# Moving the experts' input norm and slot filling into self-attention, turning the router product round, and spreading the last layer norms over the end

## The reference

```python
x = _layernorm(x + gated_linear_recurrence(x))      # Wi, Wf, Wg, scan, Wo
x = _layernorm(x + cross_attention(x, ctx))          # 32 heads, 1601 keys
x = _layernorm(x + ffn(x))
# ffn(x): causal self-attention, then experts
h = _rms(x, w_ln1); ...                              # 16 heads of 32, rotary
x = x + ctx @ wo
h = _rms(x, w_ln2)
probs = softmax(h @ w_router); top 2 of 8 experts
routed = sum of the two experts' silu(h Wg) * (h Wu) Wd, by their weight
sh = the same with a shared expert, times sigmoid(h @ w_sh_eg)
x = x + routed + sh
```

## Time and profile before

| | us |
|---|---|
| median of 2 runs (2838.88 to 2840.54) | 2839.71 |
| the profiled execution | 2848.1 |
| its span, first to last instruction | 2846.2 |
| PE busy | 2557.4 |
| DVE busy | 1292.0 |
| ACT busy | 1386.4 |

### The profile page before, as it was taken

The page is one execution under the profiler, slowest core; times in us unless marked ns, Lnnn a source line. Parts: engine busy times, 40 slices in busy tenths (PEclk is TensorE's granted clock), DMA queues, the critical chain, the costliest instruction groups (busy, mean ns, idle before and its releaser), DMA issues. The chain is left out here.

```text
span 2846.2 us, 39040 instructions
## 1 busy us (share of the span) xinstructions
PE 2557.4 (90%) x15648; PEld 1591.7 (56%) x15648; DVE 1292.0 (45%) x1943; ACT 1386.4 (49%) x1691; POOL 826.0 (29%) x489
## 2 busy tenths in 40 slices
PE   7996869999999999999968999985699988889996
PEld 5874624443444344432235556544577888888775
DVE  5666723333333333320035565542434566666574
ACT  3221046667666766689964334323312355545221
POOL 2225735441544154410014333311330011111130
PEclk9997979999999999999989999996699999999998
DMA  4002646554554545364421000005451265565330
GB/s 163 15 1 87 201 102 169 151 141 98 154 159 121 125 125 168 100 152 114 114 72 55 1 1 1 1 1 219 158 203 32 96 208 198 200 214 184 111 107 30
DMA packets 205683, 323.98 MB, mean 114 GB/s; under 512 B 68800, under 2 KB 122048, under 8 KB 203456
## 3 DMA queue, kind: packets, MB, share of 16 engines
q1 hardware_dynamic: 190448, 253.46, 30.8%
q0 software_dynamic: 15056, 68.03, 6.8%
HBM read 217.82 MB, written 103.61 MB: 113 GB/s over the span
## 5 line engine op out<-in xcount | busy, mean ns | idle before, releaser
L698 ACT ACTIVATE c_prob<-c_psum 128x1024 f32<-128x1024 f32 x832 | 815.1, 1036 | 292.6 <-PE c_psum L852 212.7
L676 POOL TENSOR_TENSOR c_rr<-c_ms,c_half 128x32 f32<-128x32 f32 x68 | 372.8, 5484 | 399.2 <-DVE c_ms L712 399.2
L869 PE MATMUL c_psum<-c_prob,c_vq 128*17 128x512 f32 x3328 | 439.7, 600 | 5.3 <-DVE c_oT L796 4.2
L852 PE MATMUL c_psum<-c_qq,c_kq 64*128 64x512 f32 x1664 | 329.9, 462 | 19.6 <-DMA c_kq<-kd 18.7
L852 PEld LDWEIGHTS c_psum<-c_qq,c_kq 64*128 64x128 f32 x1664 | 134.5, 186 | 249.4 <-ACT c_prob L698 206.5
L118 PE MATMUL m_psum<-m_t_hi,m_up_hi 128*128 128x256 f32 (+1 forms) x552 | 162.6, 295 | 41.0 <-DVE m_t_lo L1897 41.0
L118 PE MATMUL c_psum<-c_w_hi,c_c_hi 128*128 128x512 f32 x416 | 183.7, 442 | 0.2 <-DVE c_t_lo L765 0.2
L1166 DVE TENSOR_REDUCE s_topx<-s_psum 128x4 f32<-128x2048 f32 (+1 forms) x64 | 95.5, 1493 | 183.0 <-PE s_psum L1253 183.0
L118 PE MATMUL m_psum<-m_h_hi,m_up_hi 128*128 128x512 f32 (+1 forms) x384 | 154.4, 402 | 15.8 <-DVE m_work L1864 12.3
L737 DVE COPY c_raw<-c_psum 128x512 f32<-128x512 f32 x68 | 47.0, 691 | 263.6 <-PE c_psum L118 253.9
L118 PE MATMUL c_psum<-c_w_hi,c_c_lo 128*128 128x512 f32 x416 | 166.1, 399 | 0.0
(11 more groups left out here) (278 smaller groups left out, 4990.7 us busy)
## 6 DMA issues: line engine op xcount, KB each, us to landing
c_kq<-kd SPq DMA_DIRECT2D x256, 208.0 KB, 6.4
c_qq<-qd SPq DMA_DIRECT2D x64, 256.0 KB, 3.3
vd<-c_vt SPq DMA_DIRECT2D x52, 272.0 KB, 2.3
c_vq<-vd SPq DMA_DIRECT2D x32, 442.0 KB, 5.4
c_c_raw<-in_ctxT SPq DMA_DIRECT2D x52, 256.0 KB, 4.5
kd<-c_t_hi SPq DMA_DIRECT2D x52, 256.0 KB, 2.3
kd<-c_t_lo SPq DMA_DIRECT2D x52, 256.0 KB, 3.1
m_hs<-slots SPq DMA_DIRECT2D x23, 512.0 KB, 4.1
```

Of the source, the lines that this page charges most:

```text
L676: pool.tensor_tensor(rr[:, job % 2, :], ms[:, job % 2, :], half[:], ALU.pow).then_inc(s_r, 1)
L698: act.activation(prob[:, lt % 2, 2 * (u % 2):2 * (u % 2) + 2, :], score_banks[u % 3], ACT.Exp, scale=XD ** -0.5).then_inc(s_ex, 1)
L852: mm = pe.matmul(score_banks[u % 3][:, s, :], kq[rows, q % 2, u % 2, lt % CT * P:(lt % CT + 1) * P], qq[rows, q % 2, u % 2, :], start=True ...
L869: mm = pe.matmul(o_bank[32 * j:32 * j + VW, :], vq[:, q % 2, kt, j, :], prob[:, lt % 2, j, :], start=kt == 0, stop=kt == CT - 1)
```

## The change

It does four things. (1) Self-attention fills `slots` by three DRAM-to-DRAM copies of the input x, makes x + s in `xs` and 2x + s in X from each O item, takes squares, mean, root and scale of x + s there, and stores the result to `hx`; H items move one part earlier, O items 0 and 1 both to kt = 3 of c = 1. Norms of both kinds share `ss`, `ms` and `rr` in the order `roots`. (2) The experts' block no longer normalises, zeroes or adds x0: it loads `hx` batch by batch into one of two buffers. (3) The router weights, padded to 72 columns, are PE's weights and `h` moves; the [16, 512] result is copied by DVE (`take_turned`), turned back by four transposes (`turn_logits`) and copied again. The up/gate weights of stage 0 are split between batches. The comparison tiles `above` and `equal` are bf16 and lie elsewhere, so ACT no longer waits for the mask before pass 0. (4) Batch 2's last norm moves into the last pass; batch 3's statistics follow each token tile, and each token tile of it is stored on its own.

The diff, cut to its core (`split_up` and `split_down` on DVE only move up; `x_in` has two buffers; semaphores and the call sites follow):

```diff
+    def scale(self, s_each=None):
...
+            ins = self.dve.tensor_scalar(xt, xt, self.mv[:, t, 0:1], self.rstd[:, t:t + 1], ALU.subtract, ALU.mult)
+            if s_each is None:
+                self.own.done(ins)
+            else:
+                ins.then_inc(s_each, 1)
...
-                if c in (1, 2) and kt >= 2 and b:
-                    early.append(self.item("O", b - 1, 2 * (c - 1) + kt - 2))
+                if c == 1 and kt == 3 and b:
+                    early += [self.item("O", b - 1, t) for t in range(2)]
+                if c == 2 and kt >= 2 and b:
+                    early.append(self.item("O", b - 1, kt))
...
-                if c == 1 and kt >= 2 and b + 1 < B:
-                    late += [self.item("H", b + 1, 2 * (kt - 2) + k) for k in range(2)]
+                if c == 1 and kt in (1, 2) and b + 1 < B:
+                    late += [self.item("H", b + 1, 2 * (kt - 1) + k) for k in range(2)]
...
+        self.roots = [("H", 0), ("H", 1), ("H", 2), ("O", 0), ("H", 3), ("O", 1), ("O", 2), ("O", 3)]
...
-            sp.dma_start(x0.rearrange("p (t n) -> p t n", t=B * TT), X[:]).then_inc(s_saved, 16)
+            for at in range(0, SLOTS, B * T):
+                rows = min(B * T, SLOTS - at)
+                sp.dma_start(slots[at:at + rows], d["x"][0:rows]).then_inc(s_filled, 16)
+            for b in range(B):
+                for t in range(TT):
+                    sp.wait_ge(s_xs, line.root("O", b) * TT + t + 1)
+                    sp.dma_start(hx[(b * TT + t) * P:(b * TT + t + 1) * P], xs[:, t]).then_inc(s_hx[t], 16)
+            for t in range(TT):
+                sp.wait_ge(s_hx[t], 16 * B)
+            sp.wait_ge(s_filled, 16 * -(-SLOTS // (B * T)))
...
+                if n % KC == 2 and n // KC + 1 < B:
+                    inverse_root("H", n // KC + 1)
+                if n % KC == 1 and n // KC >= 2:
+                    inverse_root("O", n // KC - 2)
...
+            for b in (B - 2, B - 1):
+                inverse_root("O", b)
...
+                    if u or t:
+                        act.wait_ge(s_ss, u * TT + t)
+                    if u and t == 0:
+                        act.wait_ge(s_ms, u)
+                    if kind == "O":
+                        act.wait_ge(s_x1, b * TT + t + 1)
+                    src = X[:, b * TT + t] if kind == "H" else xs[:, t]
+                    junk = xs[:, 0] if u == 0 else unused
+                    act.activation(junk, src if u == 0 else src.rearrange("p (h n) -> p h n", h=HPC), ACT.Square, accum_out=ss[:, t:t + 1]).then_inc(s_ss, 1)
...
+            def normalise(kind, b, ts):
+                u = line.root(kind, b)
+                act.wait_ge(s_ss, u * TT + TT)
+                apart(act, s_r, u + 1, s_apart)
...
+                    if kind == "H" and b > 2:
+                        act.wait_ge(s_hx[t], 16 * (b - 2))
+                    src = X[:, b * TT + t] if kind == "H" else xs[:, t]
+                    act.activation(xs[:, t], src, ACT.Copy, scale=rr[:, t:t + 1]).then_inc(s_xs, 1)
...
+                    if c == 1 and kt < 2 and b + 1 < B:
+                        normalise("H", b + 1, (2 * kt, 2 * kt + 1))
...
-                        squares(b + 1, (2 * kt, 2 * kt + 1))
-                    if c == 1 and kt < 2 and b + 1 < B:
-                        normalise(b + 1, (2 * kt, 2 * kt + 1))
+                        squares("H", b + 1, (2 * kt, 2 * kt + 1))
+                    if c == 2 and kt == 0 and b:
+                        squares("O", b - 1, (0, 1))
+                    if c == 3 and kt == 0 and b:
+                        squares("O", b - 1, (2, 3))
+                    if c == 3 and kt >= 2 and b:
+                        normalise("O", b - 1, (2 * kt - 4, 2 * kt - 3))
                 if n + 1 < STEPS:
                     take(line.turn[n + 1])
             high_output(STEPS - 1)
+            squares("O", B - 1, range(TT))
+            normalise("O", B - 1, range(TT))
...
                     dve.wait_ge(s_put, item.index + 1)
-                    dve.wait_ge(s_saved, 16)
-                    dve.tensor_tensor(X[:, q], X[:, q], src, ALU.add).then_inc(s_x, 1)
+                    if item.n + 2 < B:
+                        dve.wait_ge(s_put, line.find("H", item.n + 2, KC - 1).index + 1)
+                    if item.n:
+                        dve.wait_ge(s_hx[item.i], 16 * item.n)
+                    dve.tensor_tensor(xs[:, item.i], X[:, q], src, ALU.add).then_inc(s_x1, 1)
+                    dve.wait_ge(s_x1, item.nth)
+                    dve.scalar_tensor_tensor(X[:, q], X[:, q], 2.0, src, ALU.mult, ALU.add).then_inc(s_x, 1)
...
+                    if c == 3 and kt == 0 and b:
+                        mean("O", b - 1)
...
-    WR = 16
+    WR = 72
+    LG = 16
...
             for b in range(B):
-                if b:
-                    sp.wait_ge(s_add, b)
-                sp.dma_start(x_in[:], x0.rearrange("p (t n) -> p t n", t=B * TT)[:, b * TT:(b + 1) * TT, :]).then_inc(s_in, 16)
-                for t in range(TT):
-                    sp.wait_ge(s_xs, b * TT + t + 1)
-                    sp.dma_start(hx[(b * TT + t) * P:(b * TT + t + 1) * P], xs[t]).then_inc(s_hx[t], 16)
+                if b >= 2:
+                    sp.wait_ge(s_T, (b - 1) * KC)
+                sp.dma_start(x_in[:, b % 2], hx[b * T:(b + 1) * T].rearrange("(t p) n -> p t n", p=P)).then_inc(s_in[b % 2], 16)
                 if b == 0:
-                    sp.wait_ge(s_zero, 1)
-                    for n in range(0, SLOTS // P, 4):
-                        r = min(4, SLOTS // P - n)
-                        sp.dma_start(slots[n * P:(n + r) * P].rearrange("(p r) n -> p (r n)", r=r), zeros[:, 0:r * H]).then_inc(s_zeroed, 16)
-            sp.wait_ge(s_T, B * KC)
-            for t in range(TT - 1):
-                sp.wait_ge(s_hx[t], 16 * B)
+                    sp.dma_start(w2[:], d["w2"]).then_inc(s_ld, 16)
+                    sp.dma_start(wr[:], d["wr"].rearrange("(k p) n -> p k n", p=P)).then_inc(s_ld, 16)
+                if b == 1:
+                    for j in range(2):
+                        load_half(0, j)
...
-            for b in range(B):
-                sp.wait_ge(s_fin, b + 1)
+            for b in range(B - 1):
+                sp.wait_ge(s_fin, TT * (b + 1))
                 sp.dma_start(out[b].rearrange("(t p) n -> p t n", p=P), X[:, b * TT:(b + 1) * TT, :]).then_inc(s_out, 16)
-            sp.wait_ge(s_out, 16 * B)
+            for t in range(TT):
+                sp.wait_ge(s_fin, TT * (B - 1) + t + 1)
+                sp.dma_start(out[B - 1, t * P:(t + 1) * P], X[:, (B - 1) * TT + t, :]).then_inc(s_out, 16)
...
-            for b in range(B):
-                pool.wait_ge(s_xs, b * TT + TT)
-                if b < B - 1:
-                    inverse_root(b + 1)
-                pool.wait_ge(s_in, b * 16 + 16)
-                pool.tensor_tensor(X[:, b * TT:(b + 1) * TT, :], X[:, b * TT:(b + 1) * TT, :], x_in[:], ALU.add).then_inc(s_add, 1)
-
...
             for b in range(B):
-                if b:
-                    act.wait_ge(s_ms, b)
-                for t in range(TT):
-                    act.activation(sig, X[:, b * TT + t, :], ACT.Square, accum_out=ss[:, t:t + 1]).then_inc(s_ss, 1)
-                    apart(act, s_ss, b * TT + t + 1, s_apart)
-            for b in range(B):
-                apart(act, s_r, b + 1, s_apart)
-                for t in range(TT):
-                    if b:
-                        act.wait_ge(s_T, b * KC)
-                        act.wait_ge(s_hx[t], 16 * b)
-                    act.activation(xs[t], X[:, b * TT + t, :], ACT.Copy, scale=rr[:, t:t + 1]).then_inc(s_xs, 1)
                 for k in range(KC):
...
-            for j in range(2):
-                split_up(0, j)
+                if b in (1, 2):
+                    split_up(0, b - 1)
...
-            act.wait_ge(s_mask, 1)
...
+                dve.tensor_tensor(dn_lo[:], dn_raw[:], dn_hi[:], ALU.subtract).then_inc(s_dnlo, 1)
+
+            def take_turned(b):
+                dve.wait_ge(s_lg, b + 1)
+                if b >= 2:
+                    dve.wait_ge(s_lT, b - 1)
+                dve.tensor_copy(turned[:, b % 2], r_bank[b % 2][0:LG, :]).then_inc(s_lt, 1)
...
             def take_logits(b):
-                dve.wait_ge(s_lg, b + 1)
-                dve.tensor_copy(logit[:, b * TT:(b + 1) * TT, :], r_bank[b % 2][:, 0:TT * WR].rearrange("p (t n) -> p t n", t=TT)[:, :, 0:NR]).then_inc(s_lc, 1)
+                dve.wait_ge(s_lT, b + 1)
+                dve.tensor_copy(logit[:, b * TT:(b + 1) * TT, :], l_bank[b % 2][:, 0:TT * LG].rearrange("p (t n) -> p t n", t=TT)[:, :, 0:NR]).then_inc(s_lc, 1)
...
                     dve.scalar_tensor_tensor(h_lo[b][:, k, :], h_bank[k], w2[:, k:k + 1], h_hi[b][:, k, :], ALU.mult, ALU.subtract).then_inc(s_hlo, 1)
+                    if b and k == 1:
+                        take_turned(b - 1)
+                if b in (1, 2):
+                    split_up(0, b - 1)
```

(43 more changed lines are left out.)

149 lines of the change are left out of this document (63 added, 86 removed).

## The result

| | before | after | |
|---|---|---|---|
| first timing, median of 2 runs each | 2839.71 | 2796.78 | ratio 0.9849, 95% interval 0.9806 to 0.9891 |
| later timing, 9 and 5 runs | 2842.74 | 2793.38 | ratio 0.9829, 95% interval 0.9808 to 0.9849 |
| span of the profiled execution | 2846.2 | 2796.9 | 49.3 less |

The forecast was 2793 with a range of 2780 to 2813, and "within 2%" at 0.85. Both timings stay within 2%.

The account below looks back on a forecast made before the run. PE was taken to bound self-attention, and a chain of hand-overs the router phase. Terms 5.5 + 7.6 - 12.2 - 33.5 - 3.5 - 10.5 = -46.6 us took 2839.7 to 2793, range 2780 to 2813.

Parts of the forecast that it names:

- 1, self-attention: Inside self-attention: extra DVE and ACT work per O item and the new order in c = 1, +5.5 us (0 to 12).
- 2 and 3, the hand-over: End of self-attention, last norm and its stores, +7.6 us; start of experts' block, until PE's first transposition, -12.2.
- 4, the router batches: Four router batches, first transposition to last logits: 69.1 us becomes 35.6, -33.5 (-36 to -26).
- 5: From the last logits to pass 0's third product: 23.3 us becomes 19.9, -3.5 (-4.5 to 0).
- wide products instead of narrow ones should keep it up: In the router batches: the clock stays up with wide products; 2.6 us added for products at the lower level.
- The rule on transposes: Router batches: transposes don't count as PE busy, so each router starts at 1.2 GHz; +6 us, about 2799.
- 6: Scatter and passes: they shift together as before, 0 us.
- 7, the end: End of the kernel: batch 2's norm in the last pass, a store per tile, -10.5 us (-12 to -7).
- 3.2 us followed the last landing before: Kernel end: the span ends 3.2 us after the last store lands, giving 2835.7 instead of 2846.2.
- cold clock and dear self-attention: Rival: router products run at 1.2 GHz (+8) and self-attention pays 12 instead of 5.5; 2807, chance 0.20.
- Batches wait for loads: Rival: hx batches queue behind 1.4 MB of weights, three waits of 4 us give back 12; 2805, chance 0.07.
- the slow copy: Rival: DRAM-to-DRAM copies into slots delay the end of self-attention; at 22 GB/s the time is 2882, chance 0.03.

Follow-up runs that it names:

- fill_only: Before with only the zeroing of slots replaced by DRAM copies of x inside self-attention; 2827.76, ratio to before 0.9953.
- copy_twice: After with the three copies into the slots done twice, 24.1 MB in place of 12.1; 2793.28, ratio to before 0.9838.
- router_narrow: After with the router's products as before, 48 of 16 columns in place of 12 per 512 tokens; 2818.72, ratio to before 0.992.
- wr_later: After with the router weights waited for where they are used, not before batch 0's transposes; 2792.72 (one run).

## Why the prediction was right

**1, self-attention, +5.5, measured +6.4.** The mechanism is the one named, and by waits of PE alone it came out closer still: 5.3 were added up and 5.1 measured. The parts are the exponential's wait at kt = 2 of c = 1 for batches 1 to 3 (three more of the 1.11 that batch 0 has in the earlier trace rows), T behind the double addition (three times 1.5), and the last `weighted` (3.2 for 2.4), less batch 0's wait before T (1.1 before, 0.3 after). The other 1.3 us fit a fall of the clock, which the prediction kept among its rivals ("each fall costs some 2 us"), but not in this sum. The extra work on ACT and DVE hides. That the copies cost nothing is shown twice (fill_only, copy_twice).

**2 and 3, the hand-over, +7.6 and -12.2, measured +7.4 and -12.6.** Both were built of rows of the same instructions, and came out within half a microsecond. "What is late next is DMA latency" is right, but it was the small load that was late, not the 1 MB of `hx`, and 1.6 us of it could be had (wr_later).

**4, the router batches, -33.5, measured -33.6** (by the landmarks; see 5). Two steps inside it don't hold. "21.6 of it the wait behind the zeroing and the stores" has no row behind it: 21.59 is PE's wait before 1961.40, where this stretch begins, and inside it ACT was idle for 19.38. PE waited 12.4, and fill_only gained 13.2. It did no harm, since the new time was built up from its own parts and not by taking 21.6 off the old. And "wide products instead of narrow ones should keep it up" is half right. They did not hold the clock up, yet they had it more often: a granted clock of 0.82 over stretch 4, against 0.59 with narrow products in router_narrow. The granted clock by stretch in after (columns as the earlier trace rows) goes up and down within the batches:

```profile
1959.00:1968.00 9.00, 7.20 (x25) 5.28 (x26) 3.19 (x5) 2.75 (x4) 0.00 (x0) 0.50 0.88 313
...
1970.00:1982.00 12.00, 7.21 (x50) 5.29 (x48) 8.86 (x13) 7.21 (x10) 0.00 (x0) 1.00 0.58 213
1982.00:1986.00 4.00, 4.00 (x13) 2.30 (x12) 1.03 (x2) 0.00 (x0) 0.00 (x0) 0.57 0.49 175
```

It was 0.50 (1.2 GHz) in batch 0's transposes and first nine products, 1.00 (2.4 GHz) after that, and fell to 0.57 inside batch 2's unbroken row of products, although PE had not been idle for more than 1.5 us at a time. A wide product is spaced 0.23 us apart at the one level and 0.43 at the other, so 17 slow ones cost 3.4 us; the allowance was 2.6. Other executions of the same router have the slow products elsewhere: copy_twice in its second and third batch, wr_later only in its second, 6 in all.

The rule on transposes of the Trainium skill that the prediction weighed (page "TensorE: Matmul & The Clock Gate", section "Part 4: PE-mode transpose") would have every router start low; batches 1, 2 and 3 started theirs behind 16 transposes at 0.40 to 0.46 us a product, the upper level, so it isn't borne out here. In copy_twice and wr_later batch 0's router, too, started at the upper level, though nothing but 16 transposes stood between it and a wait of over 14 us.

**5, -3.5, measured -4.8.** The seam was put wrong, not the work. The forecast's 19.9 us began at the end of the last router product; the landmark, the last copy of logits, comes 1.4 later. From the product (1993.4 in after) to 2013.32 it was 19.9. What was over-sized is term 4: to its own end, 1993.4, it took 34.2 us and not 35.6, in spite of the dearer clock. The part of it that was too large is the 5.4 us from a later batch's first transposition to its first product, which measured 4.72 three times. The scan waited 0.8 us for PE, so PE still ends this part, as said.

**6, 0, measured -0.5**, with a scatter that is larger (below).

**7, the end, -10.5, measured -8.3.** The norm of batch 2 fits into the last pass, as forecast: undone, it costs 8.3. DVE's part was right: its last scaling ended 5.2 us after the start of the last addition, as the forecast's 2830.2 has it. The step that failed is "3.2 us followed the last landing before": it took the landing as what the end hangs on, and so put 5.5 us behind the scaling, where 7.8 passed, as before. What the end hangs on is POOL's DRAIN. The last of four stores landed 1.5 us sooner behind its issue than one of 1 MB, and SP waited 1.6 longer for the others.

The rival "cold clock and dear self-attention" was wrong in size, though half true in kind: the clock did fall, for 17 products and not 48, and once more in self-attention. "Batches wait for loads" shows no wait of PE for `hx` behind batch 0, "the slow copy" none at all: 12.1 MB were in place at about 1527, 41 us after their issue.

What was luck is how near the plain total came. The forecast's span, 2799.6, lies 2.7 above the measured one, but 3.3 of the measured gain is scatter ahead of the change. Its time, 2793, lies 3.8 below the first timing and on the second, because the profiled execution of before was 8.4 us above its median and that of after 1.9.

## What to carry to other kernels

Build the time of a stretch from the waits of the engine that the stretch hangs on: a wait of 19.4 us on ACT was worth 13.2, because PE worked through a third of it. For small products choose the side that moves many columns; 12 products of 512 columns replaced 48 of 16 and gave 22 us, the largest piece of this change, by the estimate above about half of it through the clock. And at the end of a kernel ask which engine's queue the others wait for, in the sequencers' rows too, before making the stores finer: four stores in place of one gave nothing here.
